# Gathers in a loop from a small index buffer, with SyncE handing ring groups back, in a four-layer graph network

## What is computed

```python
# layer 0: attention, 4 heads, then two batch norms and a feed-forward
feat = xl[src] + xr[dst]; feat = where(feat >= 0, feat, 0.2 * feat)
logits = einsum('ehc,hc->eh', feat, att)       # softmax over the edges of each dst
out = segment_sum(alpha[:, :, None] * xl[src], dst)
# layer 1: relational, both directions, a weight per edge
out = segment_sum(w[:, None] * support[col], row) + segment_sum(w[:, None] * support[row], col)
# layer 2: two graph convolutions
agg = segment_sum(x[src] @ W_msg + b_msg, dst); out = agg + x @ W_self + b_self
# layer 3: attention, 8 heads
e = s_u[src] + s_v[dst]; ...; out = segment_sum(xh[src] * probs[:, None, :], dst)
```

## Time and profile before

| | us |
|---|---|
| median of 3 runs | 10865.6 |
| lowest, highest | 10844.58, 10889.47 |
| the profiled execution's own time | 10864.05 |
| its span in the trace | 10862.3 |

### The profile page before, as it was taken

The page is one execution under the profiler, slowest core; times in us unless marked ns, Lnnn a source line. Parts: engine busy times, 40 slices in busy tenths (PEclk is TensorE's granted clock), DMA queues, the critical chain, the costliest instruction groups (busy, mean ns, idle before and its releaser), DMA issues. The chain is left out here.

```text
span 10862.3 us, 133142 instructions
## 1 busy us (share of the span) xinstructions
PE 6182.5 (57%) x24674; PEld 4882.1 (45%) x24675; DVE 5021.5 (46%) x12212; ACT 1331.7 (12%) x3940; POOL 5577.6 (51%) x4923
## 2 busy tenths in 40 slices
PE   4798885774656666644444555555555532222565
PEld 2687874553544444433333344344434432222454
DVE  6444446886544444445554222242222311114888
ACT  2111111221322222200000000010000300000000
POOL 3656550000068888876665677747777156662000
PEclk9778777997877777766766677777776655555798
DMA  4555555553067777754443333323333156663354
GB/s 151 171 163 172 166 159 189 168 170 97 2 115 104 104 104 105 105 128 129 129 130 97 96 89 86 90 80 88 89 89 88 57 169 194 190 194 100 124 169 155
DMA packets 835111, 1359.28 MB, mean 125 GB/s; under 512 B 112278, under 2 KB 488660, under 8 KB 834980
## 3 DMA queue, kind: packets, MB, share of 16 engines
q0 software_dynamic: 315328, 634.04, 26.3%
q1 hardware_dynamic: 385684, 562.46, 16.0%
q10 hardware_dynamic: 133968, 161.50, 4.7%
HBM read 943.05 MB, written 414.50 MB: 125 GB/s over the span
## 5 line engine op out<-in xcount | busy, mean ns | idle before, releaser
L993 POOL DMA_INDIRECT rows_in<-table,gidx x2352 | 2471.9, 1051 | 1241.6 <-issue 646.6
L1090 PE MATMUL ps_p<-rows_in,hot 128*128 x5280 | 1767.9, 494 | 1671.2 <-DVE regionC L956 555.3
L1090 PEld LDWEIGHTS ps_p<-rows_in,hot 128*128 128x128 f32 x5280 | 1245.8, 247 | 2154.4 <-issue 1944.2
L1711 POOL DMA_INDIRECT scatter_sums<-regionC,idx x880 | 1386.5, 1576 | 307.1 <-issue 247.8
L956 DVE TENSOR_TENSOR regionC<-regionC,ps_p 128x257 f32 (+2 forms) x1320 | 558.4, 423 | 1537.1 <-DVEq L953 968.2
L1453 PE MATMUL ps_p<-regionA 128*128 128x265 f32 (+1 forms) x3520 | 965.8, 434 | 429.5 <-DVE regionB L956 197.6
L1002 POOL DMA_INDIRECT regionC<-table,gidx x784 | 807.8, 1030 | 674.7 <-POOLq L1001 440.9
L993 POOL DMA_INDIRECT regionB<-table,gidx x784 | 830.3, 1059 | 570.1 <-POOLq L991 340.4
L1453 PEld LDWEIGHTS ps_p<-regionA 128*128 128x128 f32 x3520 | 732.9, 213 | 662.0 <-DVE regionB L956 242.9
L1914 PE MATMUL psS<-dst_scores,regionA 128*128 x1760 | 393.3, 362 | 884.7 <-PEq L1912 464.2
L1914 PEld LDWEIGHTS psS<-dst_scores,regionA 128*128 128x128 f32 x1760 | 383.5, 330 | 894.5 <-issue 894.5
(11 more groups left out here) (302 smaller groups left out, 7577.9 us busy)
## 6 DMA issues: line engine op xcount, KB each, us to landing
regionA<-edge_rows SPq DMA_DIRECT2D x880, 256.0 KB, 3.3
edge_rows<-regionB SPq DMA_DIRECT2D x196, 512.0 KB
edge_rows<-regionC SPq DMA_DIRECT2D x392, 256.0 KB
regionC<-srcrow_d SPq DMA_DIRECT2D x220, 256.0 KB
scatter_sums<-zero_rows ACTq DMA_DIRECT2D x8, 6400.0 KB, 42.3
regionA<-scatter_sums ACTq DMA_DIRECT2D x49, 1024.0 KB
rows_in<-table,gidx POOLq DMA_INDIRECT x2352
regionB<-rrow_d ACTq DMA_DIRECT2D x110, 256.0 KB
```

Of the source, the lines that this page charges most:

```text
L993: g.indirect_dma_start(out=rows_of(k % (ring * EG)), out_offset=None, in_=table, in_offset=bass.IndirectOffsetOnAxis(ap=gidx[:, k:k + 1], ...
L1090: x = te.matmul(ps[(u.c * VG + j) % NB][:, 0:width], hot[:, b, 2 * j + k, :], at_tile(G, slot[j] * 2 + k), start=k == 0, stop=k == 1)
L1711: g.indirect_dma_start(out=scat, out_offset=bass.IndirectOffsetOnAxis(ap=idx[:, b, j:j + 1], axis=0), in_=sums[:, b, j, :], in_offset=None ...
```

## The change

GpSimd's gathers become a loop in all five phases. At the start of a group GpSimd waits for `ring_free[b]` (in fetch 3 `free3[b]`), copies the group's index columns from `gidx` to a small buffer `idx` of one slot per ring group, waits for that copy, and issues the group's gathers from there. The wait until a ring group is used goes from GpSimd to SyncE: `landed_groups` now also loads the visit's number, waits for it and hands the group back, half a ring behind the landing. In fetch 3 SyncE's `release` runs three groups behind in place of one.

```diff
-        group_free = sem('s_group_free')
+        ring_free = [sem(f's_ring_free{b}') for b in range(RG0)]
...
-        def landed_groups(sp, s_rows, ring, keep=None):
+        def landed_groups(sp, s_rows, used, unused, ring, keep=None, kept=None):
+            behind = ring // 2
+            regs = registers(sp, 'by_visit', 1)
...
-            for t_ in turns(sp, NEG, ring, 0):
-                group(t_.at(0))
-
-        def gather(g, name, table, rows_of, s_rows, ring, used, unused, kept=None):
+
+            def release(u):
+                b = u.c % ring
+                done = of_visits(sp, visits_by[0:1, :], u.val, regs, NV)[0]
+                if kept:
+                    kept(u, b)
+                sp.wait_ge(used.sem, done + (used.base + unused))
+                sp.sem_inc(ring_free[b], 1)
+            for b in range(ring):
+                sp.sem_inc(ring_free[b], 1)
+            for t_ in turns(sp, NEG, ring, behind):
+                if t_.has(0):
+                    group(t_.at(0))
+                if t_.has(behind):
+                    release(t_.at(behind))
...
+        def index_columns(g, u, ring, per, idx):
+            b = u.c % ring
+            g.tensor_copy(idx[:, b, :], gidx[:, bass.ds(u.val * per, per)]).then_inc(own_p, 1)
+            g.wait_ge(own_p, 1)
+            g.sem_inc(own_p, -1)
+            return [idx[:, b, j:j + 1] for j in range(per)]
+
+        def gather(g, table, rows_of, s_rows, ring, per, free, idx):
             top_row = g.to_reg(NP - 1)
-            regs = registers(g, f'by_visit_{name}', VG)
-            for n in range(NEG):
-                b, old = (n % ring, n - ring)
-                if old >= 0:
-                    if old % VG == 0:
-                        done = of_visits(g, visits_by[0:1, :], old, regs, NV)
-                    g.wait_ge(used.sem, done[old % VG] + (used.base + unused))
...
-                for k in range(n * EG, n * EG + EG):
-                    g.indirect_dma_start(out=rows_of(k % (ring * EG)), out_offset=None, in_=table, in_offset=bass.IndirectOffsetOnAxis(ap=gidx[:, k:k + 1], axis=0), bounds_check=top_row, oob_is_err=True).then_inc(s_rows[b].sem, 16)
...
+
+            def fetch(u):
+                b = u.c % ring
+                g.wait_ge(free[b], 1)
+                g.sem_inc(free[b], -1)
+                rows = index_columns(g, u, ring, per, idx)
+                for j in range(per):
+                    g.indirect_dma_start(out=rows_of(b * per + j), out_offset=None, in_=table, in_offset=bass.IndirectOffsetOnAxis(ap=rows[j], axis=0), bounds_check=top_row, oob_is_err=True).then_inc(s_rows[b].sem, 16)
+            for t_ in turns(g, ET // per, ring, 0):
+                fetch(t_.at(0))
...
+                idx = sb('gather_rows', [P, RG, EG], I32, ctx)
...
-                        landed_groups(sp, s_rows, RG)
+                        landed_groups(sp, s_rows, s_add, NB, RG)
...
-                        gather(g, name, table, lambda k: G[:, k, 0:D], s_rows, RG, s_add, NB)
+                        gather(g, table, lambda k: G[:, k, 0:D], s_rows, RG, EG, ring_free, idx)
...
-                        for t_ in turns(sp, NG3, R3, 1):
+                        behind = R3 // 2
+                        for t_ in turns(sp, NG3, R3, behind):
                             if t_.has(0):
                                 keep(t_.at(0))
-                            if t_.has(1):
-                                release(t_.at(1))
+                            if t_.has(behind):
+                                release(t_.at(behind))
...
-                        gather_eights(g, T4, lambda k: G[:, k, :], s_rows, R3, free3)
+                        gather(g, T4, lambda k: G[:, k, :], s_rows, R3, GS, free3, idx)
```

More of the change, by code:

```diff
@@ L974, in group @@
                 sp.sem_inc(s_landed.sem, 1)
-            for t_ in turns(sp, NEG, ring, 0):
-                group(t_.at(0))
-        def gather(g, name, table, rows_of, s_rows, ring, used, unused, kept=None):
-            top_row = g.to_reg(NP - 1)
-            regs = registers(g, f'by_visit_{name}', VG)
-            for n in range(NEG):
-                b, old = (n % ring, n - ring)
-                if old >= 0:
-                    if old % VG == 0:
-                        done = of_visits(g, visits_by[0:1, :], old, regs, NV)
-                    g.wait_ge(used.sem, done[old % VG] + (used.base + unused))
[L987 to L991, removed]
-                for k in range(n * EG, n * EG + EG):
-                    g.indirect_dma_start(out=rows_of(k % (ring * EG)), out_offset=None, in_=table, in_offset=bass.IndirectOffsetOnAxis(ap=gidx[:, k:k + 1], axis=0), bounds_check=top_row, oob_is_err=True).then_inc(s_rows[b].sem, 16)
@@ new lines, in landed_groups @@
+            for b in range(ring):
[5 more added lines that the diff above has]
+                    release(t_.at(behind))
+            for b in range(ring):
+                sp.wait_ge(ring_free[b], 1)
+                sp.sem_inc(ring_free[b], -1)
+        def index_columns(g, u, ring, per, idx):
[4 more added lines that the diff above has]
+            return [idx[:, b, j:j + 1] for j in range(per)]
@@ L1217, in attention_fetch0 @@
                 feat = sb('feat', [P, 2, 2 * D], F32, ctx)
+                idx = sb('gather_rows', [P, RG0, EG], I32, ctx)
                 featT = sb('featT', [P, 2, 4, P], F32, ctx)
@@ L1234, in keep, with kept @@
                             sp.dma_start(Eb[bass.ds(u.val * 2, 2), :, :].rearrange('a p c -> p a c'), G[:, b * EG:(b + 1) * EG, :].rearrange('p (a k) c -> p a (k c)', k=2)).then_inc(s_keep[b].sem, 16)
-                        landed_groups(sp, s_rows, RG0, keep)
-                        for b in range(RG0):
-                            sp.wait_ge(s_keep[b].sem, len(range(b, NEG, RG0)) * 16 + s_keep[b].base)
+                        def kept(u, b):
+                            sp.wait_ge(s_keep[b].sem, (u.val - b) // RG0 * 16 + 16 + s_keep[b].base)
+                        landed_groups(sp, s_rows, s_used, 0, RG0, keep, kept)
                     @block.gpsimd
                     def _(g):
-                        def kept(g, n, b):
-                            g.wait_ge(s_keep[b].sem, (n - b) // RG0 * 16 + 16 + s_keep[b].base)
-                        gather(g, 'att0', T0, lambda k: G[:, k, :], s_rows, RG0, s_used, 0, kept)
+                        gather(g, T0, lambda k: G[:, k, :], s_rows, RG0, EG, ring_free, idx)
                     @block.scalar
@@ L1858, in attention_fetch3 @@
                 psS = [bank(f'psS{b}', ctx) for b in (0, 1)]
+                idx = sb('gather_rows', [P, R3, GS], I32, ctx)
                 with phase() as block:
```

## The result

The changed kernel takes 10770.1 us (five runs, 10746.1 to 10775.71) against 10865.6 us (10844.58 to 10889.47): 0.9907 of before, 95% interval 0.9892 to 0.9921. It is faster by 0.9%, where 11134 us was forecast. The profiled execution took 10752.12 us, and its span is 10750.4 us.

The account below looks back on a forecast made before the run. It took TensorE to bound fetch 0 and GpSimd's issuing the passes and fetch 3. Stage changes of 0, +44, +112, +114 and 0 us gave 10864 + 270 = 11134 us, range 10870 to 11400.

Parts of the forecast that it names:

- Where the bound lies: By stage: TensorE sets fetch 0, busy 1201 of 1400 us; GpSimd is fullest in the passes and fetch 3.
- The added price: GpSimd, per group: index copy and its wait add 0.85 us, with ends at 0 and 1.17.
- Absorption: GpSimd's ring waits: two thirds usable to hide the added time, leaving +270 us over the five stages.
- Its signs of being wrong: First idle time per group under 0.6 us, passes under 1215 us, or either fetch moving by over 50 us.
- SyncE's part: SyncE's added register load, wait for use and hand-back: users never need the held signal, so no cost.
- the loop: GpSimd's register work and loop branch run ahead while the previous gather is busy, costed at nothing.
- Fetch 3's lag at 0: Fetch 3: release lag goes from 1 to 3 groups and stores issue earlier; effect put at 0.
- The rival "Faster": All stages: pauses let late results through, ring waits vanish, sum -86 us, 10778 us; chance 0.09.
- The two rules: Skill rules set aside: taken branches stall for fetch; one-hots block GpSimd copies, 14 us in each of passes 2 and 3.

Follow-up runs that it names:

- line_pause: Kernel before, straight-line, GpSimd's own ring waits, clamped, plus an unread index copy and its wait before each group's gathers: 10796.59 us, 0.9835 of before.
- loop_turn_copy: Changed kernel, clamped, with one copy and wait for a whole turn of the ring in place of one per group: 10976.57 us, 1.0005 of before.
- ctl_after: Changed kernel with the visit and group numbers it waits for clamped at 0 in a register: 10797.5 us, 0.9839 of before.
- ahead: Changed kernel, clamped, with each group's index columns copied one group ahead: 10106.42 us, 1.0127 of before, which takes 9977.75 us on that chip.
- ahead_2: Same kernel as ahead against the kernel before on a chip where that takes 10961.67 us: 10991.48 us, 1.0030 of before.

## Why the prediction was wrong

By its steps:

- **Where the bound lies**: right for the passes and fetch 3, where GpSimd's issuing was the fullest. Fetch 0 was put down to TensorE; after the change it runs at GpSimd's pace, as the passes do, and only fetch 3 still has ring waits.
- **The added price**, 0.85 us per group: somewhat too high. The break adds 0.69 us, as 0 + 0.19 + 0.80 - 0.30 in place of 0 + 0.14 + 1.01 - 0.30. The gathers got longer too (850.3 us in pass 2 against 835.6), and the whole cost where nothing hides it was 0.89 us.
- **Absorption**: this step failed. "GpSimd waits because the users are late, and they work on while it copies, so part of the added time takes the place of waiting", with two thirds of the waits usable and no stage allowed to get shorter. It took the users' lateness as given. Their lateness was itself made by GpSimd: line_pause took nothing away and added only the break, and all ring waits of the passes went. The forecast by stage was 0, +44, +112, +114 and 0 us; measured were -150, -34, +89, +91 and -75. The smaller price, 0.16 x 196 = 31 us, could account for the 23 us that passes 2 and 3 are off; it can't for the 150, 78 and 75 us of fetch 0, pass 1 and fetch 3, which got shorter than before. Fetch 0 was not bound by TensorE's 1201 us either, for TensorE was busy 1117 us after.
- **Its signs of being wrong**: the idle time before a group's first gather stayed over 0.6 us (0.80), but pass 1 took 1189 us, under 1215, and both fetches moved by over 50 us.
- **SyncE's part** and **the loop** at nothing: right, by loop_turn_copy (1.0005) and line_pause.
- **Fetch 3's lag at 0**: not settled. From its seventh group on, fetch 3 took 1153.8 us before, 1129.2 with the break alone and a lag of one (line_pause), and 1114.4 with a lag of three (ctl_after), so about 25 us of that gain would be the break's and 15 the lag's, each from single profiles of a stage that differ by up to 20 us; the lag was not tried alone.
- **The rival "Faster"**, given 0.09, had the mechanism and the size: fetch 0, the passes and fetch 3 at -164, +154 and -76 us against -150, +146 and -75, 10778 us against 10770. line_pause and loop_turn_copy show its mechanism for the passes and fetch 0 (1253 and 1433 us). For fetch 3 the match is luck: its late results stayed, and from the seventh group on, where the rival counted its 76 us, the stage went from 1137 to 1092, by 44; the other 31 us came before that. I put it low because "a pause of a microsecond is a fifth of the stop after which they moved". The rows showed that results moved after a stop; they said nothing of how short a stop would do, and 0.71 us did. The prediction held the evidence that dependences did not explain, and still treated the waits as ordinary slack.
- **The two rules.** The stall at a taken branch of the Trainium skill, "Runtime: NRT & Kernel Launch", Instruction fetch mechanics, shows in no run as a sum: the changed kernel's loops with the clamp take 10797.5 us, and the straight-line code of line_pause 10796.59 on the same chip. The other one, of "SBUF — State Buffer" in the Trainium skill, Who interferes with whom, holds here. Of the 196 copies in pass 2, 177 take 0.25 us or less and 19 more, up to 1.26 us, and all 19 run beside VectorE's one-hot; they end with it, as this pair of the changed kernel's timeline does, at 6266.1:

```profile
6264.86 1.22 DVE L941 TENSOR_TENSOR hot<-iota,rel 128x1024 f32<-128x1024 f32 x1
6264.90 1.23 POOL L998 COPY gather_rows<-gidx 128x4 int32 x1
```

  These are 10% of the copies where 12% was worked out, and 50.5 us for all copies against 196 x 0.19 = 37: some 13 us, for the 14 given. The rule was right, and nothing in the sum hung on it. The gathers are held in the same way: in pass 2 of the kernel before 74 of 784 took over 1.1 us, up to 2.06, and all 74 ran beside a one-hot, so the trace of before had the rule in it, though no row that was read.

## What to carry to other kernels

When engines wait up to 25 us for a result whose record has long ended, that is no slack to hide work in: ask what else runs in that time, and try a break in it. Where GpSimd issues indirect gathers without a break, put its other small work (index copies) between groups rather than in one block, and try the spacing stage by stage: the full break costs 0.7 to 0.9 us where GpSimd sets the pace. Time a kernel whose stages are ruled by such waits on more than one chip before choosing; here the same edit gave 0.983 to 0.991 in five sets of runs, and the runs point to 1.07 on the chip of the sixth.

## What the runs showed of the hardware

- In five of the six sets of runs (before at 10866 to 10975 us) results of TensorE came up to 26 us late while GpSimd issued gathers of 1.0 us with 0.30 us between them; in one (before at 9978 us) they did not, in the passes and fetch 3 of the four kernels profiled. The stages' lengths account for most of that tenth: 856 of the 885 us between ahead and ahead_2, the same kernel.
- Gathers did this and scatters did not: in the scatter stage of the kernel before, 880 indirect writes of 1.58 us each with the same 0.30 us between them, no result of TensorE was held for over 0.1 us. Why gathers and not scatters, and by what path, is open.
- VectorE's one-hot held a GpSimd copy of 0.19 us for up to 1.26 us (above), and gathers too: one of the changed kernel that started 0.14 us into a one-hot took 1.96 us in place of 1.01, and all 75 of the 784 in its pass 2 that took over 1.1 us ran beside one.
- A break of 0.48 us or less at the start of every four gathers does not end the lateness. One of 0.71 us filled with copies ends nearly all of it in passes 2 and 3, not in pass 1 (345 us held); one of 0.99 us ends it in all three. Every eight gathers, 0.99 us is not enough on such a chip (411 us held in pass 2, and fetch 3 as before); every 24 it does nothing (880). Whether it is the length of a break or the time added per gather is open.
